# One pool of PSUM banks, matmul waits by pass, a scan tile read in place and a new order: a change to an attention and Mamba-2 kernel

## The chip, the cores and the metric

The kernel runs on one core of one Trainium2 chip. The metric is device time in microseconds (us) for one execution; lower is better. Five engines work side by side, each through its own list of instructions in order: PE (TensorE, matmuls, with its weight loads shown as PEld), DVE (VectorE), ACT (ScalarE), POOL (GpSimd) and SP (SyncE, which here only starts DMAs). They meet through semaphores alone.

## The reference

An image batch of 4 x 128 channels x 32 x 32 goes through two layers. The first is a group norm (8 groups), single-head attention over the 1024 positions with 128 channels, a projection and a residual. The second is a layer norm over channels, a Mamba-2 core, a squeeze-and-excite gate and a residual:

```python
h = _group_norm(x, gn_w, gn_b); q, k, v = split(h @ qkv_w.T + qkv_b)
x = proj(softmax(q k^T / sqrt(128)) v) + x
u = layernorm(x) * norm_g + norm_b;  z, xBC, dt = split(u @ in_w.T)
dt = softplus(dt + dt_bias);  xs, Bm, Cm = split(silu(causal_conv4(xBC) + conv_b))
state = state * exp(dt * A) + (dt * x_t) B_t;   y_t = state C_t      # 1024 steps, 4 heads
y = rmsnorm((y + Dp * xs) * silu(z)) * rms_w;   out = y @ out_w.T
return x + out * sigmoid(se2 @ relu(se1 @ mean(out)))
```

All data is float32.

## The kernel before

**Tiling.** Batches are named a to d. The 1024 positions of a batch are 8 tiles of 128, or two halves of 512. Attention runs over the 8 query tiles: `S` (scores of a tile against one half of the keys, three passes of 512 columns in the faster f32r format, from a high and a low part of each operand: hi x hi, lo x hi, hi x lo), `max` on DVE, `exp` on ACT, `T` (transposes on PE), `pT` (their copy on ACT) and `PV` (on PE). Step numbers run over tile and half: `S5a` is tile 2, half 1 of batch a. `Q` makes the queries of a half, in three passes as well; `q_hi` (ACT) and `q_lo` (DVE) split them into high and low parts.

**Mamba.** The scan over 1024 steps is done in chunks of 128, four in each half. Per half: `UT`, `u` (the normed input, transposed), `InX`, `InBC`, `InZ`, `Dt` (input projections on PE), `conv_*`, `term` and `th_*` (the convolution and silu, on ACT, POOL and DVE), `sp` (nine small DVE steps for softplus), `Cum`, `dec`, `dA`, `DAT` and `l` (the decays), `xdt`, `xend`, `BT`, `G`, `m` (operands and masked scores inside a chunk), `U` (what each chunk adds to the state, PE), `st` (DVE's scan over the four chunks), `stc` (ACT's copy of the scan's result), `Yo` (what earlier chunks give to the output, PE), `Y` (inside the chunk, PE), `yo`, `yo_dx`, `y`, `g` (the sum and the gate), `sq`, `Ss`, `ms`, `y_pow` (the rms norm), `Out`, `o`, `Pl`, `SeA`, `SeB`, `gated`, `fin`, `store`. In batch d the decays come from matmuls (`Dec`, `L`); in a to c they go through DRAM (`wr`, `bc`, `dd` on SP's queue).

**The scan's layout.** `U` writes its bank with a step of four columns, so that the four chunks of one state column lie side by side; `st` scans along them into `scanned[128, 2, 128, 4]`. `stc` (L772) reads that with a step of four elements and writes `stateT[128, 2, 4, 128]`, in which each chunk's state is contiguous. `Yo` (L1333) loads `stateT` as weights, and the second half's `U` (L1317) reads the last chunk of the first half from it, as the moving operand against an identity.

**What sets the order.** One list of step names, `ORDER` (L62 to L138), is written out by hand. Every engine walks the whole list and emits its own steps, so each engine's queue follows that order; the waits of each step are in the code. `name@2` names the PSUM bank that a PE step fills.

**PSUM.** Eight banks: two for `scores` (also the target of `Q`), two `turn` banks for `V` and `T`, one for `attn_out` (`PV`), and three `mamba` banks for all other steps (L175 to L178). `fill` (L378) makes PE wait until the bank's last content was read; it looks this up in two tables, one for each pool.

**Waits of the three passes.** `mm3` (L1159) issues three matmuls in a row. `S` (L1214) and `Q` (L1199) wait for all operands, low parts included, ahead of the first pass.

**Head.** DVE first copies the identity four times (`ident4`), makes `center`, and then the masks that batch d needs (L834 to L842, the last of them behind a wait for all of POOL's constants). Only then do the group norm's statistics of batch a start (`gn_stats`, L883). `gn_dev` is a copy of the group means from PSUM and three small steps (L897 to L900); after `gn_ve` and `gn_pow` comes `gn_aff`, three more (L908 to L910).

## Time and profile before

| what | before |
|---|---|
| three runs | 275.29, 275.69, 276.14 us (median 275.69) |
| the profiled execution's own time | 275.25 us |
| its span, first to last instruction | 273.1 us |
| PE busy | 256.9 us (94%), 1992 matmuls |
| DVE busy | 224.8 us (82%), 517 instructions |
| ACT busy | 208.5 us (76%), 414 instructions |
| POOL busy | 109.0 us (40%), 114 instructions |

PE's busy time is modelled: a matmul's record reaches past the start of the next one, so a PE that is shown busy may still lose some tenths of a microsecond between steps. Where it does, the weight loads (PEld) show an idle time with what ended it. In the profile's rows a line number is a line of the kernel; `L1157` is the helper that issues every matmul, so matmuls are told apart by their tiles (out <- in, moving operand first, weights second). A 32-bit matmul shows as two records, and an f32r matmul as one.

### The profile page before, as it was taken

The numbers are of one execution on the slowest core, as the hardware profiler recorded it, in microseconds if no ns is written. First come the engines' busy times: TensorE is split into PE (matmuls) and PEld (weight loads), VectorE is DVE, ScalarE is ACT, GpSimd is POOL, SyncE is SP. The second block draws the span as 40 slices with busy tenths as digits, with TensorE's granted clock in tenths as the row PEclk, the third lists the DMA queues.
The fourth block names the chain that finished last, engine by engine and source line by source line (L and its number), as shares of the span: only waits on it lengthen the run. The fifth ranks groups of instructions, "written<-read, shape, count | busy, mean of one in ns | idle before, by whom it ended". The sixth has DMA issues, their size and how long they took to land. (4 is left out here: it accounts for less than half of the span.)

```text
span 273.1 us, 6193 instructions
## 1 busy us (share of the span) xinstructions
PE 256.9 (94%) x1992; PEld 224.3 (82%) x1992; DVE 224.8 (82%) x517; ACT 208.5 (76%) x414; POOL 109.0 (40%) x114
## 2 busy tenths in 40 slices
PE   2999999999999999999999998999999999998791
PEld 2889998998888998989989787888889788677680
DVE  5787765754889799889988999999899999599933
ACT  2356579978999887879999875777978888997261
POOL 8030032208053300642387534132463188556162
PEclk9999999999999999999999999999999999999996
DMA  6930000006000600000326000060007201000014
GB/s 175 397 136 4 0 0 4 0 5 186 8 0 6 183 12 2 0 2 0 112 78 206 0 2 1 16 182 2 0 5 189 84 0 42 0 2 1 0 41 155
DMA packets 10987, 15.29 MB, mean 56 GB/s; under 512 B 1515, under 2 KB 5708, under 8 KB 10956
## 3 DMA queue, kind: packets, MB, share of 16 engines
q1 hardware_dynamic: 10412, 14.69, 16.7%
q8 instruction: 17, 0.28, 0.4%
q10 hardware_dynamic: 544, 0.21, 0.3%
q14 instruction: 14, 0.11, 0.2%
HBM read 12.70 MB, written 2.20 MB: 55 GB/s over the span
## 5 line engine op out<-in xcount | busy, mean ns | idle before, releaser
L1157 PEld LDWEIGHTS attn_out<-values,pT 128*128 128x128 f32 x512 | 63.3, 191 | 5.8 <-issue 4.0
L1157 PE MATMUL attn_out<-values,pT 128*128 128x129 f32 x512 | 66.7, 276 | 0.0
L974 DVE TENSOR_REDUCE neg_max<-scores 128x1 f32<-128x1024 f32 x32 | 39.0, 1218 | 16.0 <-PE scores L1157 15.8
L649 ACT ACTIVATE probs<-scores,neg_max 128x512 f32<-128x512 f32 x64 | 41.8, 685 | 13.1 <-DVE neg_max L974 11.1
L655 ACT ACTIVATE pT<-turn 128x512 f32<-128x512 f32 x64 | 37.6, 595 | 10.8 <-PE turn L1230 10.8
L1230 PE MATMUL turn<-ident,probs 128*128 128x128 f32 x256 | 37.1, 273 | 0.0
L575 POOL TENSOR_TENSOR pre<-pre,th 128x512 f32<-128x512 f32 x16 | 21.4, 1336 | 30.0 <-ACT pre L681 18.3
L1230 PEld LDWEIGHTS turn<-ident,probs 128*128 128x128 f32 x256 | 30.2, 142 | 2.9 <-issue 0.7
L1157 PE MATMUL scores<-h_hi,q_hi 128*128 128x512 f32 x64 | 30.4, 474 | 0.0
L1067 DVE TENSOR_TENSOR_SCAN L<-L,ident 128x512 f32<-128x512 f32 x24 | 29.9, 1256 | 0.0
L561 POOL TENSOR_TENSOR ln_rstd<-ln_var,neg_half 128x4 f32<-128x4 f32 x8 | 9.8, 1230 | 47.6 <-DVE ln_var L996 47.5
L1157 PE MATMUL scores<-h_hi,q_lo 128*128 128x512 f32 x64 | 25.3, 395 | 0.0
L1157 PE MATMUL scores<-h_lo,q_hi 128*128 128x512 f32 x64 | 25.1, 392 | 0.0
L1157 PE MATMUL mamba<-u,winC 128*128 128x512 f32 x48 | 24.5, 597 | 0.1
L1081 DVE TENSOR_TENSOR L<-L,mamba 128x512 f32<-128x512 f32 x32 | 21.0, 675 | 0.0
L1013 DVE SCALAR_TENSOR_TENSOR pre<-raw,vec,pre 128x512 f32<-128x512 f32 x21 | 17.8, 849 | 0.1
L582 POOL TENSOR_TENSOR xend<-xdt,to_end 128x512 f32<-128x512 f32 x8 | 8.7, 1089 | 22.0 <-issue 16.5
L588 POOL TENSOR_TENSOR xs<-y,gate 128x512 f32<-128x512 f32 x7 | 10.0, 1423 | 18.4 <-DVE y L1122 18.3
L593 POOL TENSOR_TENSOR y_rstd<-ms,neg_half 128x4 f32<-128x4 f32 x8 | 10.1, 1260 | 15.5 <-DVE ms L1125 15.5
L1157 PEld LDWEIGHTS scores<-h_hi,q_lo 128*128 128x128 f32 x64 | 12.0, 188 | 2.7
L1157 PEld LDWEIGHTS scores<-h_hi,q_hi 128*128 128x128 f32 x64 | 12.1, 189 | 2.6 <-issue 0.9
L776 ACT ACTIVATE stateT<-scanned 128x512 f32<-128x512 f32 x8 | 9.3, 1164 | 5.6 <-DVE scanned L1089 5.6
(219 smaller groups left out, 592.4 us busy)
## 6 DMA issues: line engine op xcount, KB each, us to landing
L<-decay_rows_d SPq DMA_DIRECT2D x24, 256.0 KB, 3.9
res<-in_x_tok SPq DMA_DIRECT2D x4, 512.0 KB, 7.8
out<-res SPq DMA_DIRECT2D x8, 256.0 KB, 2.7
x_all<-in_x SPq DMA_DIRECT2D x3, 512.0 KB, 8.5
decay_in<-decay_rows_d SPq DMA_DIRECT2D x24, 64.0 KB, 3.5
x_all<-in_x SPq DMA_DIRECT2D x2, 256.0 KB, 3.2
winT<-in_in_wT SPq DMA_DIRECT2D x1, 194.0 KB, 7.2
wqkv<-in_qkv_w ACTq DMA_DIRECT2D x1, 192.0 KB, 4.1
```

The lines of the kernel that those rows point to most:

```text
L561: pool.tensor_tensor(ln_rstd[:, four], ln_var[:, four], neg_half[:, four], ALU.pow).then_inc(ln_rstd_ready.sem, 1)
L575: pool.tensor_tensor(pre[:, 1, half_of(n)], pre[:, 1, half_of(n)], term(b, n, j), ALU.add).then_inc(tap["bc"].sem, 1)
L588: pool.tensor_tensor(y2[:, half], y[:, half], gate[:, half], ALU.mult).then_inc(y2_ready.sem, 1)
L593: pool.tensor_tensor(y_rstd[:, four], ms[:, four], neg_half[:, four], ALU.pow).then_inc(y_rstd_ready.sem, 1)
L649: act.activation(probs[:, i % 2, half_of(h)], scores[:, half_of(h)], ACT.Exp, bias=neg_max[:, i:i + 1]).then_inc(exp_done.sem, 1)
L655: act.activation(pT[:, i % 2, QUAD * h:QUAD * (h + 1), :], bank[:, :].rearrange("p (a b) -> p a b", a=QUAD), ACT.Copy).then_inc(pT_ready.s ...
L974: V.tensor_reduce(neg_max[:, n:n + 1], scores[:, :], AX.X, ALU.max, negate=True).then_inc(max_ready.sem, 1)
L1013: V.scalar_tensor_tensor(pre[:, 0, half_of(n)], raw[:, 0, n * HALF + j:(n + 1) * HALF + j], vec[:, CONV_X + j:CONV_X + j + 1], pre[:, 0, h ...
L1067: V.tensor_tensor_scan(chunk, chunk, ident4[:, :, :].rearrange("p a b -> p (a b)"), 0.0, ALU.mult, ALU.add).then_inc(l_ready.sem, 1)
L1081: V.tensor_tensor(M[:, HEADS * n:HEADS * (n + 1), :], L[:, HEADS * n:HEADS * (n + 1), :], bank[:, tile(c)].unsqueeze(1).broadcast_to([P, H ...
L1157: return T.matmul(o, w, v, start=start, stop=stop)
L1230: last = T.transpose(bank[:, tile(c)], probs[:, i % 2, tile(QUAD * h + c)], ident[:, :])
```

## The change

1. **Head.** The masks move out of the head of DVE's list: a new step `masks0` keeps `ident4` and `center`, `masks1` takes the rest and stands behind `q_lo0a`. `gn_dev` reads the group means in PSUM directly, and for batch a fuses two steps; `gn_aff` makes the bias in one step, not two. `kq_ev` moves behind `gn_pow`, `vp_mm` behind the five warm-up matmuls.
2. **Waits by pass.** `mm3` is gone. Each pass of `Q` and `S` has the waits of its own operands: the low part of the keys (`h_lo`) only ahead of the pass that reads it, `q_lo` only ahead of the last.
3. **One pool of banks.** `turn` and `mamba` become five banks for every step, and `Q` fills one of these too, not `scores`. `fill` looks up what read the bank last in one table.
4. **No copies of the states.** `stc` and `stateT` are gone. `Yo` loads its weights from `scanned` with a step of four elements (16 bytes), and the second half's `U` reads its moving operand so; both wait for `st`, and the next batch's `st` waits for `Yo` and `U`.
5. **Order anew.** `ORDER` is rewritten as a whole: the same steps, without `stc` and with `masks`, in another order and with other banks.

On SP's queue the new order puts both halves' `bc` loads ahead of the `dd` loads of batches a and b.

The core of the diff (the order's table shows two lines only):

```diff
@@ ORDER @@
-warm3 gn_stats0 gn_mm10 kq_mm gn_dev0 gn_mm20 kq_ev gn_ve0 vp_mm gn_pow0 gn_aff0 h0a h1a warm5 h_hi0a h_hi1a h_lo0a
+masks0 warm3 gn_stats0 gn_mm10@2 kq_mm@3 gn_dev0 gn_mm20 gn_ve0 gn_pow0 kq_ev gn_aff0 h_hi0a h_hi1a warm5 h0a vp_mm@4
...
-        turn = [ctx.enter_context(nc.psum_tensor(f"turn{k}", [P, HALF], F32)) for k in range(2)]
         attn_out = ctx.enter_context(nc.psum_tensor("attn_out", [P, HALF], F32))
-        mb = [ctx.enter_context(nc.psum_tensor(f"mamba{k}", [P, HALF], F32)) for k in range(3)]
+        pool_banks = [ctx.enter_context(nc.psum_tensor(f"bank{k}", [P, HALF], F32)) for k in range(5)]
...
         def fill(pe, b, kind, n):
-            uses, memory = (TURN_USES, turn) if kind in ("V", "T") else (MAMBA_USES, mb)
+            uses, memory = USES, pool_banks
             bank, before = uses[kind, n, b]
             if before is not None:
...
+                for read, batch, count in released(*before):
+                    wait(pe, read, batch, count)
             return memory[bank], filled[kind].sem
...
-                elif kind == "stc":
-                    wait(act, st_ready, b, n + 1)
-                    wait(act, filled["Yo"], b - 1, n + 1)
-                    wait(act, filled["U"], b - 1, 2)
-                    act.activation(stateT[:, n, :, :], scanned[:, n, :, :].rearrange("s e c -> s c e"), ACT.Copy
-                                   ).then_inc(stc_ready.sem, 1)
...
                 elif kind == "gn_dev":
-                    step_done(V.tensor_copy(gn_mean[:, b0:b1], mb[2][:, b0:b1]))
-                    step_done(V.tensor_tensor(gn_dev[:, b0:b1], gn_mv[:, b0:b1, 0], gn_mean[:, b0:b1], ALU.subtract))
-                    step_done(V.tensor_tensor(gn_dev[:, b0:b1], gn_dev[:, b0:b1], gn_dev[:, b0:b1], ALU.mult))
-                    V.tensor_tensor(gn_dev[:, b0:b1], gn_dev[:, b0:b1], gn_mv[:, b0:b1, 1], ALU.add
-                                    ).then_inc(gn_dev_done.sem, 1)
+                    bank = take(dve, 0, "gn_mm1", n)
+                    step_done(V.tensor_tensor(gn_dev[:, b0:b1], gn_mv[:, b0:b1, 0], bank[:, b0:b1], ALU.subtract))
+                    if n == 0:
+                        V.scalar_tensor_tensor(gn_sq[:, 0:1], gn_dev[:, 0:1], gn_dev[:, 0:1], gn_mv[:, 0:1, 1], ALU.mult, ALU.add
+                                               ).then_inc(gn_dev_done.sem, 1)
...
                 elif kind == "gn_aff":
-                    step_done(V.tensor_tensor(gn_bias[:, b0:b1], gn_mean[:, b0:b1], gn_scale[:, b0:b1], ALU.mult))
-                    V.tensor_scalar(gn_bias[:, b0:b1], gn_bias[:, b0:b1], -1.0, vec[:, GNB:GNB + 1], ALU.mult, ALU.add
-                                    ).then_inc(gn_ready.sem, 1)
+                    for k in range(b0, b1):
+                        last = V.scalar_tensor_tensor(gn_bias[:, k:k + 1], gn_minus_mean[:, k:k + 1], gn_scale[:, k:k + 1],
+                                                      vec[:, GNB:GNB + 1], ALU.mult, ALU.add)
...
                 elif kind == "st":
-                    wait(dve, stc_ready, b - 1, n + 1)
+                    wait(dve, filled["Yo"], b - 1, n + 1)
+                    if n == 0:
+                        wait(dve, filled["U"], b - 1, 2)
...
                 elif kind == "S":
                     i, h = divmod(n, 2)
                     if i == 0:
-                        wait(pe, q_lo_ready, b, h + 1)
+                        wait(pe, q_hi_ready, b, 1)
+                        wait(pe, exp_done, b - 1, 15 + h)
                     else:
                         wait(pe, exp_done, b, n - 1)
+                        wait(pe, q_hi_ready, b, i // QUAD + 1)
+                    wait(pe, h_hi_ready, b, h + 1)
+                    mm(to, q_hi[:, tile(i)], h_hi[:, keys], True, False)
+                    wait_h_lo(pe, b, h + 1)
+                    mm(to, q_hi[:, tile(i)], h_lo[:, keys], False, False)
                     wait(pe, q_lo_ready, b, i // QUAD + 1)
-                    wait_h_lo(pe, b, h + 1)
-                    mm3(scores[:, half_of(h)], q_hi[:, tile(i)], q_lo[:, tile(i)], h_hi[:, half_of(h)],
-                        h_lo[:, half_of(h)]).then_inc(S_filled.sem, 1)
+                    mm(to, q_lo[:, tile(i)], h_hi[:, keys], False, True).then_inc(S_filled.sem, 1)
...
                 elif kind == "U":
                     if n == 1:
-                        wait(pe, stc_ready, b, 1)
+                        wait(pe, st_ready, b, 1)
...
-                        mm(slots[:, 0, :], ident[:, :], stateT[:, 0, QUAD - 1, :])
+                        mm(slots[:, 0, :], ident[:, :], scanned[:, 0, :, QUAD - 1])
...
                 elif kind == "Yo":
-                    wait(pe, stc_ready, b, n + 1)
+                    wait(pe, st_ready, b, n + 1)
                     for c in range(1 - n, QUAD):
-                        last = mm(bank[:, tile(c)], stateT[:, n, c - 1 + n, :], BC[:, tile(QUAD * n + c)])
+                        last = mm(bank[:, tile(c)], scanned[:, n, :, c - 1 + n], BC[:, tile(QUAD * n + c)])
```

The order at three places. The first is the head on DVE, before (`head_mask` and `first` are masks; `gn_*` is the group norm of batch a; `key_query_*` and `col` are `kq_ev`):

```order
L839 TENSOR_TENSOR head_mask<-row_head,row_chunk 128x512
L842 TENSOR_SCALAR first<-ident 128x1
L883 BN_STATS gn_raw<-x_all 128x6 x2
L888 BN_AGGR gn_mv<-gn_raw 128x2
L897 COPY gn_mean<-mamba 128x1
L898 TENSOR_TENSOR gn_dev<-gn_mv,gn_mean 128x1
L899 TENSOR_TENSOR gn_dev<-gn_dev 128x1
L900 TENSOR_TENSOR gn_dev<-gn_dev,gn_mv 128x1
L914 TENSOR_SCALAR key_query_hi<-turn 128x128
L915 SCALAR_TENSOR_TENSOR key_query_lo<-turn,key_query_hi 128x128
L917 TENSOR_SCALAR col<-turn 128x1
L904 TENSOR_SCALAR gn_var<-mamba 128x1
```

and now:

```order
L863 TENSOR_SCALAR center<-ident 128x128
L880 BN_STATS gn_raw<-x_all 128x6 x2
L885 BN_AGGR gn_mv<-gn_raw 128x2
L894 TENSOR_TENSOR gn_dev<-gn_mv,bank 128x1
L896 SCALAR_TENSOR_TENSOR gn_sq<-gn_dev,gn_mv 128x1
L902 TENSOR_TENSOR gn_minus_mean<-gn_dev,gn_mv 128x1
L905 TENSOR_SCALAR gn_var<-bank 128x1
L917 TENSOR_SCALAR key_query_hi<-bank 128x128
L918 SCALAR_TENSOR_TENSOR key_query_lo<-bank,key_query_hi 128x128
L920 TENSOR_SCALAR col<-bank 128x1
L910 TENSOR_SCALAR gn_scale<-gn_rstd,vec 128x1
```

The masks stand ahead of the statistics no more, two small steps are gone ahead of `gn_var`, and `kq_ev` stands behind it.

The second is the same stretch on PE, before (`gn_dev,group_avg` is `gn_mm2`, `wpT` is `vp_mm`, `scores<-ident` are warm-up matmuls, the last three rows are `Q0a`):

```order
L1157 MATMUL mamba<-gn_dev,group_avg 128x1
L1157 MATMUL turn<-wpT,wqkv 128x128
L1157 MATMUL turn<-wpT,vec 128x128
L1157 MATMUL scores<-ident 128x128 x5
L1157 MATMUL scores<-h_hi,key_query_hi 128x512
L1157 MATMUL scores<-h_lo,key_query_hi 128x512
L1157 MATMUL scores<-h_hi,key_query_lo 128x512
```

and now (the last row is `V0a`):

```order
L1163 MATMUL bank<-gn_sq,group_avg 128x1
L1163 MATMUL scores<-ident 128x128 x5
L1163 MATMUL bank<-wpT,wqkv 128x128
L1163 MATMUL bank<-wpT,vec 128x128
L1163 MATMUL bank<-h_hi,key_query_hi 128x512
L1163 MATMUL bank<-h_hi,key_query_lo 128x512
L1163 MATMUL bank<-h_lo,key_query_hi 128x512
L1163 MATMUL bank<-value_proj,h 128x128 x4
```

`vp_mm` stands behind the warm-up matmuls, the pass with the low part of `h` is the last of `Q0a`, and `V0a` stands ahead of `Q1a`.

The third is DVE in batch d behind the last attention step `PV15d`, up to `dt_x1d` (`dtx`), before (`th<-xs,vec,th` is `yo_dx1c`, `y` and `ms` belong to batch c, the rest to d):

```order
L1109 SCALAR_TENSOR_TENSOR th<-xs,vec,th 128x512
L847 CAST dA_rows<-dA 128x32
L849 TENSOR_TENSOR dA_rows<-dA,dA_rows 128x32
L1122 TENSOR_TENSOR y<-mamba,th 128x512
L1125 TENSOR_SCALAR ms<-mamba 128x4
L1051 CAST dA_all<-mamba 128x128
L1052 TENSOR_TENSOR dA_head<-mamba,head_mask 128x512
L1115 SCALAR_TENSOR_TENSOR gate<-gate,zv 128x512
L1000 TENSOR_TENSOR dtx<-mamba,dtb 128x16
L1005 SCALAR_TENSOR_TENSOR dta<-dtx 128x16
```

and now (`L<-L` are `m6c` and `m7c`, `th<-bank,decay_in` is `yo1c`, `x_all` is `gated1b`):

```order
L827 CAST dA_rows<-dA 128x32
L829 TENSOR_TENSOR dA_rows<-dA,dA_rows 128x32
L1085 TENSOR_TENSOR L<-L,bank 128x512 x2
L1055 CAST dA_all<-bank 128x128
L1056 TENSOR_TENSOR dA_head<-bank,head_mask 128x512
L1107 TENSOR_TENSOR th<-bank,decay_in 128x512
L1131 TENSOR_SCALAR ms<-bank 128x4
L1146 SCALAR_TENSOR_TENSOR x_all<-th_att,y 128x512
L1115 SCALAR_TENSOR_TENSOR th<-xs,vec,th 128x512
L1128 TENSOR_TENSOR y<-bank,th 128x512
L1004 TENSOR_TENSOR dtx<-bank,dtb 128x16
```

`m6c`, `m7c`, `yo1c` and `gated1b` stand behind `PV15d` now; `yo1c` was the only one of them behind it before, and `gate0d` moved to behind `dtx`.

## Rows read from the trace of the kernel before

**Rows 1.** Windows, us: busy time (count) of PE, PEld, DVE, ACT, POOL; clock; DMA.

```profile
150.00:226.00 76.00, 74.80 (x617) 65.11 (x616) 73.34 (x158) 60.05 (x121) 32.56 (x28) 1.00 0.15 43
226.00:240.00 14.00, 13.56 (x109) 10.35 (x108) 9.77 (x36) 12.66 (x33) 9.29 (x8) 1.00 0.06 20
240.00:250.00 10.00, 9.19 (x57) 7.48 (x57) 9.88 (x17) 8.91 (x18) 7.24 (x6) 1.00 0.01 2
250.00:262.00 12.00, 9.49 (x122) 7.97 (x122) 11.25 (x19) 4.56 (x9) 2.35 (x3) 1.00 0.00 1
```

**Rows 2.** Longest waits of PE's weight loads, 12 to 226 us: total, times, longest.

```profile
PEld attn_out L1157 <- issue: 4.0, 17, 0.2
PEld mamba L1157 <- issue: 3.5, 15, 0.5
...
PEld mamba L1157 <- ACT stateT L776: 0.9, 1, 0.9
```

**Rows 3.** Timeline of the head: start, us, engine, line, operation [idle before <- releaser].

```profile
4.89 0.15 DVE L842 TENSOR_SCALAR first<-ident 128x1 f32<-128x1 f32 x1 [0.60 <-POOL sp_coef L529]
...
5.08 1.29 DVE L883 BATCH_NORM_STATS2 gn_raw<-x_all 128x6 f32<-128x512 f32 x2
...
7.28 0.16 DVE L897 COPY gn_mean<-mamba 128x1 f32<-128x1 f32 x1 [0.68 <-PE mamba L1157]
...
9.58 2.34 PE L1157 MATMUL scores<-ident 128*128 128x128 f32 x10
...
10.32 1.52 ACT L632 ACTIVATE h_hi<-x_all,gn_bias,gn_scale 128x512 fp32r<-128x512 f32 x2 [5.31 <-DVE gn_bias L910]
...
11.98 0.19 PEld L1157 LDWEIGHTS scores<-h_hi,key_query_hi 128*128 128x128 f32 x1 [0.35 <-DVE h_lo L966]
...
16.26 1.21 DVE L974 TENSOR_REDUCE neg_max<-scores 128x1 f32<-128x1024 f32 x1
```

**Rows 4.** The copied state's tile, `stateT`: duration ns min/median/max, first and last start.

```profile
L1157 PEld LDWEIGHTS mamba<-BC,stateT x56: 186/192/192, 124.2 to 258.3; 128*128 128x128 f32 x56
...
L776 ACT ACTIVATE stateT<-scanned x8: 1121/1161/1203, 122.4 to 256.3; 128x512 f32<-128x512 f32 x8
...
L1157 PE MATMUL mamba<-stateT,ident x8: 275/275/377, 127.2 to 254.1; 128*128 128x128 f32 x8
```

**Rows 5.** Groups by form: busy us, mean ns of one | idle before.

```profile
L1081 DVE TENSOR_TENSOR L<-L,mamba 128x512 f32<-128x512 f32 x32 | 21.0, 675 | 0.0
...
L712 ACT ACTIVATE C<-BC 64x512 f32<-64x512 f32 x8 | 5.0, 629 | 0.2
```

**Rows 6.** Timeline, PE alone: an f32r stream, then loads with one moving column.

```profile
19.59 0.40 PE L1157 MATMUL scores<-h_hi,q_hi 128*128 128x512 f32 x1
...
19.83 0.39 PE L1157 MATMUL scores<-h_lo,q_hi 128*128 128x512 f32 x1
...
264.31 1.93 PEld L1157 LDWEIGHTS mamba<-y_rstd,y 128*128 128x128 f32 x16
```

**Rows 7.** A wait of PE's sequencer by itself, `L1312`: duration ns min/median/max.

```profile
L1312 PEldq EVENT_SEMAPHORE  x8: 51/51/51, 86.2 to 251.1; - x8
```

**Rows 8.** Timeline from the last attention step on, PE and DVE.

```profile
225.75 1.61 PE L1157 MATMUL attn_out<-values,pT 128*128 128x129 f32 x13
...
234.40 0.17 DVE L1000 TENSOR_TENSOR dtx<-mamba,dtb 128x16 f32<-128x16 f32 x1 [1.88 <-PE mamba L1157]
...
234.72 1.10 PE L1157 MATMUL mamba<-u,winC 128*128 128x512 f32 x2
...
236.01 0.18 DVE L855 TENSOR_SCALAR sp_den<-dte 128x16 f32<-128x16 f32 x1 [0.85 <-ACT dte L725]
...
239.56 0.18 DVE L847 CAST dA_rows<-dA 128x32 fp32r<-128x32 f32 x1 [0.57 <-ACT dA L736]
...
257.57 1.16 PE L1157 MATMUL mamba<-BC,stateT 128*128 128x128 f32 x8
...
261.13 0.69 DVE L1131 TENSOR_TENSOR xs<-y,gate 128x512 f32<-128x512 f32 x1
```

313 lines of the change are left out of this document (162 added, 151 removed).

## The prediction

> **What bounds the kernel now.** I read the windows first. From 150 to 226 us, where attention and Mamba steps of three batches run side by side, PE is busy for 74.80 and DVE for 73.34 of 76 us, while ACT (60.05) and POOL (32.56) have room [rows 1]. So PE sets the pace there, with DVE 2 us behind it. Behind 226 us, where the last attention step ends at 225.75 + 1.61 = 227.36 us [rows 8], it is another kernel: DVE is idle for 14 - 9.77 = 4.2 us up to 240 us, and then busy for 21.1 of 22 us up to 262 us [rows 1]. There DVE is the bound, and PE, with 9.49 of 12 us at the end, is not.
>
> Next come PE's own waits, which its modelled busy time hides: weight loads lose 4.0 us in 17 waits ahead of `PV` and 3.5 us in 15 ahead of Mamba steps, each about 0.2 us, and 0.9 us once for the copied state [rows 2]. Last the head: queries start at 11.98 us and the first maximum at 16.26 us [rows 3].
>
> What PE has to do is the same before and after, to the instruction; the change can win only where PE waits, at both ends, and it can lose where a PE instruction gets longer.
>
> **The change, part by part.** I sum against the profiled execution's own 275.25 us, with the 2.15 us around its span left as they are; it lies 0.44 us under the median of the three runs, so I add 0.44 at the end.
>
> *Head.* `first` waits 0.60 us for POOL's last constant and the statistics follow at 5.08 us [rows 3]. Now they can start once the data are there. No row says how early that is, so this is worth 0 to 0.75 us (the wait and the 0.15 us of `first`); I take 0.5. Two of the small steps like `gn_mean` (0.16 us each, 0.2 with the gap, [rows 3]) go ahead of `gn_var`, but PE runs `kq_mm` in that gap anyway, so only 0.1 of the 0.4 us counts; the third, in `gn_aff`, saves 0.2. So `h_hi` starts 0.8 us earlier, at 9.5 instead of 10.32 us. `kq_ev` behind `gn_ve` costs nothing as long as POOL's power (`gn_pow`) takes as long; without that cover it costs its three steps, some 0.6 us. On PE the warm-up (2.34 us, [rows 3]) and `vp_mm` now stand behind `gn_mm2` and ahead of `Q0a`, so its start moves by 0.6 us, not 0.8; `Q0a` no longer waits for `h_lo` (0.35 us, [rows 3]), which is the same time seen from the other side. `masks1` then stands ahead of `max0a` on DVE and takes some of this back, but PE fills that time with `V1a` and `win_mm`, which stood behind it. I take **-0.8 us**, from 0 to -1.2.
>
> *Banks.* With five banks for all, and `Q` out of `scores`, a fill can take a bank that was read long ago. The rows do not say which of the 8.4 us of waits [rows 2] are for a bank and which for data, so this is worth 0 to 8.4 us; a new order makes waits of its own too. Short waits of 0.2 us mean that things come just late, which a freer choice cures often but not always. I take a little over a third, **-3 us**, with the 0.9 us for `stateT` in it.
>
> *No copies.* ACT loses eight copies of 1161 ns [rows 4], 9.3 us; ACT has room, so by itself that is worth nothing but latency, which is counted above. In return 56 weight loads of `Yo` and the 8 matmul records of the second `U` [rows 4] read with a step of 16 bytes. No PE row does this. The nearest by operation are PE's own: an f32r stream takes 19.83 - 19.59 = 0.24 us for 512 columns, 0.47 ns each [rows 6], while one-column matmuls go at the pace of their weight loads, 1.93 / 16 = 0.12 us for 128 columns, 0.94 ns each [rows 6]. If a step of 16 bytes costs two reads for one, there is room for it in a 32-bit load, and the cost is near 0. The nearest by memory is the copy itself: ACT needs 1161 ns for 512 elements with this step and 629 ns for 512 in a row [rows 4, 5], 1.04 ns more for each; 128 of them make 133 ns, and 64 loads 8.5 us. Less than nothing is excluded: a read in steps has no reason to beat one in a row. I take **+0.4 us**, by the PE rows, since the engine is the same, and keep 0 to 8.5.
>
> The Trainium skill (page "SBUF — State Buffer", section "Specifications (TRN2)") speaks against this part: memory lines are 16 bytes, full bandwidth needs at least two hits to a line, and each crossing to a new line pays. ACT's rows agree with it. With PE paying as ACT does, the sum below would be 277.6 us, without a penalty 270.7; that is the first rival.
>
> *Waits by pass.* In batches b to d the pass that reads `h_lo` carries two waits, and one instruction more on PE's sequencer, 51 ns [rows 7]: 48 `S` and 6 `Q`, 2.8 us if none is hidden. The pass before it runs for 0.24 us [rows 6], which covers it unless the sequencer is already late. What it gains is at most 0.35 us at each of four batch starts [rows 3], 1.4 us. I take **+0.3 us**, from -1.4 to +2.8.
>
> *Order.* Behind `PV15d` PE's list now also has `InZ0d` (1.10 us, like the pair in [rows 8]) and `Yo1c` (1.16 us, [rows 8]), while `Cum0d` (four records, 0.5 us at the pace of [rows 6]) stands ahead of it. So the last attention step comes about **1.5 us** earlier, and PE has room for the rest in the 2.5 us that it is idle from 250 to 262 us. DVE there gets `m6c`, `m7c` and `gated1b` more, 2.0 us at 675 ns [rows 5], and loses `gate0d`, which goes behind `dtx`. Their cover is DVE's wait of 1.88 us ahead of `dtx` and the two of 0.85 and 0.57 us behind it [rows 8]; without that cover they cost 2 us at the end, where DVE is the bound. But `Dt1d` stands behind `InX1d` now, so `dtx` is up to 1.1 us later. Filled idle and later start nearly cancel: 0, from -2 to +2. Removing `stc` from the end gives nothing by itself, since DVE is the bound there and `g1d` (261.13 us, [rows 8]) comes when DVE gets to it. On SP the `dd` loads of batches a and b now queue behind both halves' `bc`; `yo` reads them tens of microseconds later, so 0.
>
> Sum: -0.8 - 3 + 0.4 + 0.3 - 1.5 = -4.6. 275.25 - 4.6 + 0.44 = **271.1 us**.
>
> **The rivals.**
>
> *The step of four is paid (slower).* Each of the 64 loads takes 133 ns more. 40 of them lie ahead of `PV15d`, on PE's path: 5.3 us. Of the 24 behind (`Yo1c` 8, `Yo0d` 6, `Yo1d` 8, `U1d` 2) I count half, 1.6 us, as DVE is the bound there. 6.9 instead of 0.4 us: 277.6 us. It decides from about 96 ns for each load on, where 52 loads use up the other parts' 5.0 us. For it speaks ACT's doubled time [rows 4, 5] and that no row shows a 32-bit load of 128 columns go faster than 0.12 us [rows 6], so its spare room is not seen. Against it speaks the f32r stream, twice as fast on the same engine.
>
> *DVE binds instead.* DVE's work is the same but for three small steps, and from 150 to 226 us it has 2.7 us to spare [rows 1]. If it has none at the places where PE now waits less, PE's waits only change their names, and the 3 and the 1.5 us do not come: 275.6 us, no change. Against it: DVE itself waits for PE in places, `dtx` by 1.88 us [rows 8].
>
> *The order does more.* All of the 8.4 us of waits [rows 2] go, not 3: 265.7 us. Against it: that needs every operand on time for each of some 360 PE steps.
>
> *The change doesn't do what it says* is no case here: the order shows the copies gone and the steps moved.
>
> **How the numbers follow.** Forecast 0.52, paid step 0.19, DVE 0.17, more 0.12. A difference under 0.3% (0.8 us) can't be told from no change. Faster: 0.52 and 0.12, and a quarter of the DVE case, 0.68; same: most of the DVE case, 0.11; slower: the paid step and what is left, 0.21. The range goes from 267.0 us, which leaves out most of the third rival, to 277.0 us, which takes in half of the first.
>
> **What would show it.** In the profile after: the first `Q0a` pass at about 11.4 us and the first maximum under 16 us; the `Yo` loads at 192 ns and their matmuls 0.12 us apart (the forecast) or some 0.25 (the first rival); the waits of weight loads between 12 and 226 us down by a third; the last `PV` at about 222 us; from there to the end 45 to 47 us, as before, with DVE over 90% busy in all of its last 30 us. I would be wrong if PE's waits stay at 8 us in all, if `Yo` takes twice its time, or if DVE shows new waits behind `PV15d`.

## The result, and the profile after

| what | before | after |
|---|---|---|
| median (lowest to highest), us | 275.72 (275.29 to 276.14) | 277.71 (277.30 to 278.13) |
| ratio to before, 95% interval | | 1.0072 (1.0051 to 1.0094) |
| span of the profiled execution, us | 273.1 | 275.5 |
| PE busy, us | 256.9 | 261.4 |
| DVE / ACT busy, us | 224.8 / 208.5 | 225.1 / 200.0 |

The change makes the kernel 2.0 us slower. The forecast was 271.1 us, faster; the time lies 0.7 us above the range that was to hold it, and 0.1 us from the first rival's 277.6, which had a chance of 0.19.

PE's busy time is the first sign. It has the same 1992 instructions as before, and is busy for 4.5 us more. So some of its instructions have become longer. The rows of the scan's tile in the changed kernel show which (after the colon: lowest, median and highest duration in ns; then the first and the last start in us):

```profile
L1163 PEld LDWEIGHTS bank<-BC,scanned x56: 307/329/332, 127.2 to 260.5; 128*128 128x128 f32 x56
L1163 PE MATMUL bank<-BC,scanned x56: 270/397/499, 127.6 to 260.6; 128*128 128x128 f32 x56
L1163 PEld LDWEIGHTS bank<-scanned,ident x8: 187/189/208, 122.8 to 256.2; 128*128 128x128 f32 x8
L1163 PE MATMUL bank<-scanned,ident x8: 387/398/407, 123.0 to 256.4; 128*128 128x128 f32 x8
```

[rows 4] had 192 ns for the loads of the copied state and 275 ns for the carry's matmuls. A `Yo` load now takes 329 ns, 137 more, and the matmul behind it follows suit. In the carry the tile is the moving operand: its load (an identity, in a row) is as fast as ever, and the matmul takes 398 ns, 123 more. So both ways of reading pay for the step of four.

The stages of the changed kernel, to be read beside [rows 1] (columns: window; busy us and instruction count of PE, PEld, DVE, ACT and POOL; granted clock; DMA share; GB/s):

```profile
150.00:226.00 76.00, 76.00 (x620) 67.54 (x619) 72.74 (x154) 58.01 (x121) 35.57 (x28) 1.00 0.23 64
226.00:240.00 14.00, 13.62 (x107) 11.09 (x106) 11.69 (x31) 10.90 (x26) 9.96 (x9) 1.00 0.05 20
240.00:250.00 10.00, 9.49 (x62) 7.99 (x60) 8.08 (x23) 9.89 (x23) 5.77 (x5) 1.00 0.01 2
250.00:262.00 12.00, 11.05 (x116) 9.88 (x119) 11.46 (x21) 4.17 (x9) 6.31 (x6) 1.00 0.12 45
```

From 150 to 226 us PE is shown busy without a gap (74.80 before). From 250 to 262 us it is busy for 11.05 us, 1.6 more than before: `Yo0d`, `Yo1d` and the carry lie there.

The last `PV` of the kernel, first before, then after (start, length, engine, line; x16 and x3 are neighbours that the view has joined, two steps in the first two rows). The third row is from a kernel of the experiments, told below:

```profile
225.41 1.95 PE L1157 MATMUL attn_out<-values,pT 128*128 128x129 f32 x16
```
```profile
227.18 2.05 PE L1163 MATMUL attn_out<-values,pT 128*128 128x129 f32 x16 [0.23 <-DVE res L989]
```
```profile
223.16 2.05 PE L1163 MATMUL attn_out<-values,pT 128*128 128x129 f32 x16 [0.23 <-DVE res L989]
```

It ends at 229.23 us, where 222 was forecast and 227.36 stood before. From there to the end it is 46.3 us (45.7 before). So nearly all of the loss has come about by then.

The idle time of PE's weight loads between 12 and 226 us (what waited; for what; us in all, times, longest; "issue" means that the profile names nothing), first the rows of before that [rows 2] did not need, then after:

```profile
PEld turn L1157 <- issue: 1.0, 4, 0.2
PEld scores L1157 <- ACT probs L649: 0.4, 2, 0.2
PEld attn_out L1157 <- DVE res L985: 0.5, 2, 0.3
```
```profile
PEld bank L1163 <- issue: 4.6, 20, 0.2
PEld scores L1163 <- ACT probs L653: 1.6, 5, 0.6
PEld attn_out L1163 <- issue: 1.4, 6, 0.2
PEld bank L1241 <- issue: 1.1, 4, 0.4
PEld attn_out L1163 <- DVE res L989: 0.9, 2, 0.6
```

The waits of `PV` with no named releaser went from 4.0 us in 17 [rows 2] to 1.4 in 6, and the one of 0.9 us for the copied state is gone. Those ahead of steps that fill a bank did not change: 3.5 in 15 [rows 2] and 1.0 in 4 are 4.5 in 19; now it is 4.6 in 20. `S` waits longer for `exp` than before (1.6 against 0.4 us), and `PV` for `res` (0.9 against 0.5).

But most of the short waits with no named releaser are no loss for PE. This is one stretch of the kernel before, on PEld and then on PE (`u,winC` is an input projection of 512 columns, two records):

```profile
150.50 0.42 PEld L1157 LDWEIGHTS mamba<-u,winC 128*128 128x128 f32 x2
151.16 0.19 PEld L1157 LDWEIGHTS attn_out<-values,pT 128*128 128x128 f32 x1 [0.24 <-issue]
151.58 0.53 PEld L1157 LDWEIGHTS attn_out<-values,pT 128*128 128x128 f32 x4 [0.24 <-issue]
```
```profile
150.72 1.02 PE L1157 MATMUL mamba<-u,winC 128*128 128x512 f32 x2
151.58 0.61 PE L1157 MATMUL attn_out<-values,pT 128*128 128x129 f32 x4
```

PE streams the projection from 150.72 to 151.58 us and goes on with `PV` without a gap. The next two loads start 0.43 us apart, as the two records do, and each shows 0.24 us of idle time while PE works; so an idle time of the weight loads alone does not say, as the text ahead of the prediction took it to, that PE loses time. Of the waits with no named releaser, 32 of 49 (7.7 of 11.6 us) before and 31 of 38 (7.6 of 9.2 us) after are such first two loads behind a projection, and PE shows no idle time in any of those before. In [rows 2] they are 14 of the 17 of `PV` and 6 of the 15 of Mamba steps, 4.8 of 7.5 us. Both kernels have the same 48 records of projections; what the new order changed is which step stands behind them, and so whose name the idle time carries.

The head after, on DVE and on PE (beside [rows 3]):

```profile
3.77 0.69 DVE L880 BATCH_NORM_STATS2 gn_raw<-x_all 128x6 f32<-128x512 f32 x1 [0.84 <-DMA x_all<-in_x]
9.40 1.00 DVE L964 TENSOR_SCALAR h<-x_all,gn_scale,gn_bias 128x512 f32<-128x512 f32 x2
15.63 1.23 DVE L978 TENSOR_REDUCE neg_max<-scores 128x1 f32<-128x1024 f32 x1 [0.34 <-PE scores L1163]
```
```profile
10.73 0.77 PE L1163 MATMUL bank<-h_hi,key_query_hi 128*128 128x512 f32 x1
```

The statistics wait for the data alone, `h` (and `h_hi`, at the same time on ACT) starts at 9.40 instead of 10.32 us, `Q0a` at 10.73 instead of 11.98 [rows 3], and the first maximum at 15.63 instead of 16.26. So only half of what `Q0a` gains arrives there: from its first pass to the next step it takes 1.4 us (10.73 to 12.16) where it took 0.8 (11.98 to 12.78), at a granted clock of 1.00 in both traces; why, no run shows. In the kept traces of the seven kernels below that have this head and these waits, the first maximum comes anywhere from 15.07 to 16.03 us.

### The profile page after: what moved, and what is told of

It reads as the page before. It is cut to its first block, busy times and chain, and to the rows that moved or that the text cites. A ratio compares the mean times of both kernels' runs of the same rounds, so it can differ in the third digit from the quotient of the medians.

```text
span 275.5 us, 6187 instructions
## 1 busy us (share of the span) xinstructions
PE 261.4 (95%) x1992; PEld 232.1 (84%) x1992; DVE 225.1 (82%) x516; ACT 200.0 (73%) x406; POOL 112.4 (41%) x114
## 4 chain that ended last, share of the span: by engine, by line
PE 81%; DVE 11%; issue 3%; ACT 2%; POOL 1%; DVEq 0%; ACTq 0%; POOLq 0%
PE bank L1163 34%; PE attn_out L1163 17%; PE scores L1163 17%; PE bank L1241 9%; DVE L L1071 2%; DVE neg_max L978 2%; PE bank L1257 1%; DVE L L1085 1%; PE bank L1309 1%; PE bank L1315 1%; DVE gate L1121 0%; DVE x_all L1146 0%; DVE woutT L936 0%; DVE th L1115 0%; DVE th L1107 0%
## 5 line engine op out<-in xcount | busy, mean ns | idle before, releaser
L659 ACT ACTIVATE pT<-bank 128x512 f32<-128x512 f32 x64 | 37.5, 598 | 19.4 <-PE bank L1241 19.1
L1241 PE MATMUL bank<-ident,probs 128*128 128x128 f32 x256 | 37.4, 273 | 0.2 <-DVE q_lo L974 0.2
L1241 PEld LDWEIGHTS bank<-ident,probs 128*128 128x128 f32 x256 | 30.2, 142 | 2.7 <-issue 1.1
L579 POOL TENSOR_TENSOR pre<-pre,th 128x512 f32<-128x512 f32 x16 | 22.5, 1406 | 24.1 <-ACT pre L685 18.2
L1163 PE MATMUL bank<-u,winC 128*128 128x512 f32 x48 | 24.5, 594 | 0.0
L1085 DVE TENSOR_TENSOR L<-L,bank 128x512 f32<-128x512 f32 x32 | 20.8, 675 | 0.0
L592 POOL TENSOR_TENSOR xs<-y,gate 128x512 f32<-128x512 f32 x7 | 10.7, 1528 | 22.2 <-DVE y L1128 22.2
L559 POOL TENSOR_TENSOR h_lo<-h,h_hi 128x512 fp32r<-128x512 f32 x6 | 7.8, 1313 | 26.1 <-ACT h_hi L636 26.1
L586 POOL TENSOR_TENSOR xend<-xdt,to_end 128x512 f32<-128x512 f32 x8 | 8.7, 1088 | 23.8 <-issue 11.7
L1163 PE MATMUL bank<-BC,scanned 128*128 128x128 f32 x56 | 14.3, 396 | 0.4 <-DVE scanned L1095 0.4
L1163 PEld LDWEIGHTS bank<-BC,scanned 128*128 128x128 f32 x56 | 13.8, 326 | 1.0 <-DVE scanned L1095 0.6
```

What stands on the lines that cost most here:

```text
L579: pool.tensor_tensor(pre[:, 1, half_of(n)], pre[:, 1, half_of(n)], term(b, n, j), ALU.add).then_inc(tap["bc"].sem, 1)
L586: pool.tensor_tensor(xend[:, rows, :], xdt[:, rows, :], to_end[:, rows].unsqueeze(2).broadcast_to([P, R, HEADDIM]), ALU.mult).then_inc(xen ...
L592: pool.tensor_tensor(y2[:, half], y[:, half], gate[:, half], ALU.mult).then_inc(y2_ready.sem, 1)
L659: act.activation(pT[:, i % 2, QUAD * h:QUAD * (h + 1), :], bank[:, :].rearrange("p (a b) -> p a b", a=QUAD), ACT.Copy).then_inc(pT_ready.s ...
L1085: V.tensor_tensor(M[:, HEADS * n:HEADS * (n + 1), :], L[:, HEADS * n:HEADS * (n + 1), :], bank[:, tile(c)].unsqueeze(1).broadcast_to([P, H ...
L1163: return T.matmul(o, w, v, start=start, stop=stop)
```

## The experiments

My theory once the trace was read: the step of four is paid at every read, some 122 ns for each of 56 + 8 records (275 to 397 and 398), 7.8 us of PE's time, and what the rest of the change wins does not make up for it. The main rival: the step's time lies beside DVE's work, and the order or the banks lose the time.

**1. The changed kernel, reading in a row.** `Yo` and the carry read as many elements, 128 that lie side by side:

```diff
-                        last = mm(bank[:, tile(c)], scanned[:, n, :, c - 1 + n], BC[:, tile(QUAD * n + c)])
+                        last = mm(bank[:, tile(c)], scanned[:, n, :, :].rearrange("s e c -> s (e c)")[:, tile(c - 1 + n)],
+                                  BC[:, tile(QUAD * n + c)])
```

> The changed kernel with one difference: Yo and the second U read the first 512 elements of the scan's tile in a row instead of every fourth one (the states are the wrong ones, all else, waits and order too, is the same). Theory: the step of four is what cost the time. In the profile of the changed kernel 56 Yo loads start 0.233 us apart instead of 0.112, and the 8 carry records 0.208 instead of 0.111: 6.8 + 0.8 = 7.5 us of PE's time, of which at least the 40 loads ahead of PV15d and the first carries count in full, the rest half. So 277.7 - 5.5 to 7.5: about 271 us (270.2 to 272.2), loads back at 192 ns. Rival: the step's time lies beside DVE's work, and the new order or its banks lose the time: 276 to 277.7 us although the loads are at 192 ns.

Measured: 272.69 us, ratio to before 0.9896 (0.9861 to 0.9931). The loads are back:

```profile
L1163 PEld LDWEIGHTS bank<-BC,scanned x56: 186/192/192, 127.4 to 256.8; 128*128 128x128 f32 x56
L1163 PE MATMUL bank<-BC,scanned x56: 270/275/377, 127.8 to 256.9; 128*128 128x128 f32 x56
```

So the step cost 277.71 - 272.69 = 5.0 us, give or take one by the two intervals, and without it the change would have been a gain of 2.9 us. The rival falls.

The six runs go from 271.70 to 274.73 us, and the trace is of the slowest. There PE was busy for only 0.91 of 2 us from 222 to 224 us, and then the granted clock fell to 0.50, the lower of its two levels, 1.2 GHz, from 225 to 228 us. The last `PV` took 3.34 us in it:

```profile
224.54 3.34 PE L1163 MATMUL attn_out<-values,pT 128*128 128x129 f32 x16 [0.23 <-DVE res L989]
```

So where the time went is read below from another kernel's trace. The gain is less than the 5.0 us that the prediction's other terms add up to; the later experiments ask where that stayed.

**2. Copies straight behind the scan.** The changed kernel with `stc` back on ACT: behind each `st` of `ORDER` stands its `stc`, and `Yo` and `U` read `stateT`.

```diff
-... st0a raw_x0b ... st1a exp10c ...
+... st0a stc0a raw_x0b ... st1a stc1a exp10c ...
```

> The changed kernel with ACT's copies of the states put back (stc straight behind st on ACT, Yo and U read the copy), all other parts of the change kept. Theory (the step costs, and ACT had room for the copies): about 271 to 272.5 us, since the copies bring back 1.2 us of latency behind each scan, 0.9 us of wait at one place before. Rival (the copies' latency is worth as much as the step): 275 us or more.

Measured: 285.31 us, 1.0368 (1.0331 to 1.0404). Far off both: 12.6 us slower than reading in a row (the trace is of the fastest of its four runs, 283.02 us). ACT goes through its list in order, and `stc` there waits for DVE, which is behind. The first row of that kernel's trace is what `stc` waited for, the others what PE then waited for (12 to 226 us):

```profile
DVE scanned L1096: 11.7, 6
```
```profile
PEld scores L1164 <- ACT probs L650: 4.1, 7, 1.6
PEld bank L1242 <- issue: 4.0, 5, 2.3
```

ACT stood for 11.7 us in six waits, and `exp` and `pT`, which stood behind them, came late: `S` lost 4.1 us waiting for `exp`, where the changed kernel lost 1.6. `T` (L1242) lost 4.0 us in waits with no named releaser, where it had lost 1.1 (L1241 there); it needs `exp` and a bank that `pT` has read. Dropping ACT's copies was not worth nothing, as I had put it; with the order of the change it depends on where they would stand.

**3. The step alone, in the kernel before.** The copies are still made and waited for; only the read changes.

```diff
-                        last = mm(bank[:, tile(c)], stateT[:, n, c - 1 + n, :], BC[:, tile(QUAD * n + c)])
+                        last = mm(bank[:, tile(c)], scanned[:, n, :, c - 1 + n], BC[:, tile(QUAD * n + c)])
```

> The kernel before with one difference: Yo and the second U read the scan's tile with a step of four; the copies are still made and still waited for, so no wait and no place in the order changes. Theory: PE pays 7.5 us more, of which 5 to 7 count: 275.7 + 5 to 7 = 280.7 to 282.7 us. Rival (PE has slack at these places): under 278 us.

Measured: 282.90 us against 275.56, 1.0260 (1.0237 to 1.0283). In the old order the step costs 7.3 us, almost all of its 7.8 us of PE time. The loads show 329 ns there too. So the price does not depend on the order; how much of it is hidden does.

**4. Steps of 1, 2, 3, 4 and 8.** Each step on a line of its own, in the changed kernel:

```diff
+                        T.matmul(bank[:, tile(1)], flat[:, 0:128], BC[:, tile(1)], start=True, stop=True)
+                        T.matmul(bank[:, tile(2)], flat[:, 0:256:2], BC[:, tile(2)], start=True, stop=True)
+                        last = T.matmul(bank[:, tile(3)], flat[:, 0:384:3], BC[:, tile(3)], start=True, stop=True)
...
+                        T.matmul(bank[:, tile(2)], flat[:, 0:1024:8], BC[:, tile(6)], start=True, stop=True)
+                        last = T.matmul(bank[:, tile(3)], flat[:, 512:1024:4], BC[:, tile(7)], start=True, stop=True)
```

> The changed kernel where the reads of the scan's tile use different steps, each on a line of its own (wrong states): Yo's loads with steps of 1, 2, 3 elements in the first half and 1, 2, 8, 4 in the second; the carry's moving operand with steps of 1, 2, 3, 4 in batches a to d. If the price comes from the number of 16-byte lines touched, with two hits to a line being enough: 192 ns at steps 1 and 2, and more at 3, 4 and 8 alike, up to 329. If any step doubles the read: 329 ns at every step but 1. If the price grows with the spread of addresses: 192, about 235, 280, 329 and well over 329 at 8. The moving operand should follow the same pattern.

The loads, with steps of 1 (L1356), 2 (L1357), 3 (L1358), 8 (L1362) and 4 (L1363):

```profile
L1356 PEld LDWEIGHTS bank<-BC,scanned x8: 190/192/192, 127.1 to 251.1; 128*128 128x128 f32 x8
L1357 PEld LDWEIGHTS bank<-BC,scanned x8: 196/197/199, 127.6 to 251.4; 128*128 128x128 f32 x8
L1358 PEld LDWEIGHTS bank<-BC,scanned x8: 252/258/261, 127.9 to 251.6; 128*128 128x128 f32 x8
...
L1362 PEld LDWEIGHTS bank<-BC,scanned x8: 313/324/335, 132.8 to 255.3; 128*128 128x128 f32 x8
...
L1363 PEld LDWEIGHTS bank<-BC,scanned x8: 329/332/333, 133.3 to 255.8; 128*128 128x128 f32 x8
```

At steps of 1, 2, 3, 4 and 8 that is 192, 197, 258, 332 and 324 ns: two is nearly free, three costs half of what four costs, and eight no more than four. This is neither "any step" nor "the spread of addresses". The Trainium skill (page "SBUF — State Buffer", section "Specifications (TRN2)") says that lines are 16 bytes and that full bandwidth needs at least two hits to each; the trace agrees. Read as "an element costs one element time, and a line at least two", 128 elements in steps of 1, 2, 3, 4, 8 touch 32, 64, 96, 128, 128 lines, and take 128, 128, 192, 256, 256 element times. With 192 ns at a step of one and 329 ns at four put in (137 / 128 = 1.07 ns for an element time) that gives 192, 260 and 329 ns at two, three and eight, where 197, 258 and 324 were measured. The moving operand shows the same (steps of 2 and 3 below; 275 in a row and 398 at four are shown above):

```profile
L1340 PE MATMUL bank<-scanned,ident x2: 276/276/277, 170.0 to 170.1; 128*128 128x128 f32 x2
...
L1342 PE MATMUL bank<-scanned,ident x2: 333/338/344, 221.6 to 221.8; 128*128 128x128 f32 x2
```

**5. Copies where ACT is idle.** If the copies of the second experiment hurt only by their place, they can be put elsewhere. In the kernel that reads in a row ACT has idle stretches of one to three microseconds not long behind most scans; each copy of batches a to c goes to one of them or next to it. The first half copies the three chunks that `Yo` needs, the carry and batch d read in steps.

```diff
+                elif kind == "stc":
+                    wait(act, st_ready, b, n + 1)
+                    wait(act, filled["Yo"], b - 1, n + 1)
+                    used = QUAD - 1 + n
+                    act.activation(stateT[:, n, 0:used, :], scanned[:, n, :, 0:used].rearrange("s e c -> s c e"), ACT.Copy
+                                   ).then_inc(stc_ready.sem, 1)
```

> The changed kernel with copies again, but placed by the trace of the kernel that reads in a row: in batches a to c each copy stands where ACT was idle there, some microseconds behind the scan and not straight behind it; the first half copies only the three chunks that Yo reads. The second U reads the scan's tile in steps (2 records a batch), and batch d keeps its reads in steps. Theory (the copies cost 7.6 us in the kernel with copies straight behind the scan because ACT stood waiting for the scan, 11.7 us in 6 waits, and all behind it on ACT with it): 272.7 us of reading in a row, 0.8 to 1.7 for 14 Yo records of batch d, up to 0.8 for the carries: 273.5 us (272.7 to 275). Rival (the copies themselves are in ACT's way, 6 of about 1.1 us, or the latency of 1.2 us is): over 277 us.

Measured: 273.86 us, 0.9920 (0.9894 to 0.9946). It leaves nothing out and beats both kernels: 1.9 us under the 275.79 us of before in these runs, 3.9 under the changed one. The copies take as long as ever, but the wait for the scan is gone from their rows (what the copies waited for, below the row):

```profile
L777 ACT ACTIVATE stateT<-scanned x6: 918/1031/1131, 118.1 to 227.2; 128x384 f32<-128x384 f32 x3, 128x512 f32<-128x512 f32 x3
its engine sat idle before it (us, times) until:
  issue: 0.5, 2
```

**6. One pool in the old order.** The changed code under the list of before, copies at their old places, masks at the head; each fill gets the bank of the five that was read longest ago in the list.

```diff
-stats0c term2b max5c stc0a PV4c Yo0a@1 Cum0b@2 pT5c gate0a exp10c PV5c sp11b pT6c T7c@0 T8c@1 cd0b sp12b
+stats0c term2b max5c stc0a PV4c Yo0a@0 Cum0b@1 pT5c gate0a exp10c PV5c sp11b pT6c T7c@2 T8c@3 cd0b sp12b
```

> The code of the changed kernel (one pool, waits by pass, the shorter steps of the head) under the order of before, masks at the head, copies at their old places; the banks are given by rule, each fill the one of five that was read longest ago in the list. So no new order and no step. Prediction's terms: banks -2.1 without the 0.9 for the copied state, waits +0.3, small head steps -0.3: about 273.5 us (271.5 to 274.5). Rival (in the old order the waits are for data, not for banks): 275.6 us, no change.

Measured: 277.13 us, 1.0049 (1.0032 to 1.0066): no gain, but 1.3 us lost. The waits (12 to 226 us):

```profile
PEld bank L1164 <- issue: 5.3, 17, 1.3
PEld attn_out L1164 <- issue: 3.3, 14, 0.2
PEld bank L1316 <- issue: 1.4, 1, 1.4
```

With five banks free to all, `PV` still waits 3.3 us in 14 (4.0 in 17 before), and steps that fill a bank wait no less than before. Most of the short waits are the loads behind a projection, told above, which no choice of banks can cure. The two long ones, 1.4 and 1.3 us, are new, and PE's own rows name what ended them:

```profile
91.86 0.52 PE L1316 MATMUL bank<-ident,BC 128*128 128x128 f32 x3 [0.96 <-DVE q_lo L977]
172.72 0.46 PE L1164 MATMUL bank<-BC,stateT 128*128 128x128 f32 x2 [0.92 <-ACT pT L656]
```

In this kernel's list `BT1a` fills the bank that `Q0c` filled last, and `q_lo0c` on DVE still had to read it; `Yo0b` fills the bank of `T1d`, which `pT1d` on ACT had to read. Neither step needs these results for anything else. So, read from the list and these rows, the rule that gave out the banks made two waits for banks, and together they are more than the 1.3 us lost.

**7. Waits ahead of the first pass again.** Experiment 1, with all waits of `S` and `Q` ahead of their first pass (the diff shows `S`):

```diff
                     wait(pe, h_hi_ready, b, h + 1)
+                    wait_h_lo(pe, b, h + 1)
+                    wait(pe, q_lo_ready, b, i // QUAD + 1)
                     mm(to, q_hi[:, tile(i)], h_hi[:, keys], True, False)
-                    wait_h_lo(pe, b, h + 1)
                     mm(to, q_hi[:, tile(i)], h_lo[:, keys], False, False)
-                    wait(pe, q_lo_ready, b, i // QUAD + 1)
```

> The kernel of the first experiment (the changed one that reads in a row, wrong states) with the waits of S and Q put back ahead of the first pass. Prediction's term for waits by pass is +0.3 us from -1.4 to +2.8, so against 272.7 us: 272.4 (269.9 to 274.1). Rival: the new order counts on them, so that passes start before h_lo and q_lo are there and undoing costs more than 1.4 us: over 274.1 us.

Measured: 273.31 us, 0.9907 (0.9886 to 0.9929). Undoing them costs 0.6 us, give or take about one by the two intervals. So waits by pass can't be told from no change here; a cost of 0.3 us is not excluded.

**8. The step in batch d alone.** Batches a to c read in a row (as in experiment 1, not each chunk's own state), d in steps.

```diff
-                        last = mm(bank[:, tile(c)], scanned[:, n, :, c - 1 + n], BC[:, tile(QUAD * n + c)])
+                        last = mm(bank[:, tile(c)], scanned[:, n, :, :].rearrange("s e c -> s (e c)")[:, tile(c - 1 + n)]
+                                  if by_dma(b) else scanned[:, n, :, c - 1 + n], BC[:, tile(QUAD * n + c)])
```

> The changed kernel where only batch d reads the scan's tile in steps; a to c read in a row (wrong states). 14 Yo records at 121 ns and 2 of the carry at 97 ns more: 1.9 us of PE behind the last attention step. The prediction counted such reads by half, as DVE is the bound there: 272.7 + 0.9 = 273.6 us. If DVE hides them all: 272.7. If they lie on the path in full: 274.6. The reads of a to c then carry the rest of the 5.0 us that the step cost in all.

Measured: 273.74 us, 0.9947 (0.9924 to 0.9970), 1.05 us above reading in a row. That is half of the 1.95 us of batch d's 16 records (122 ns each), as the prediction had counted, but with the scatter of both kernels (272.98 to 275.45 us here) it may be none or all. The traces part the price better; their granted clock is 1.00 up to 262 us. Up to the last `PV` this kernel reads in a row, and that ends at 223.16 + 2.05 = 225.21 us (third row of the `PV` rows above), 4.0 us before the changed kernel's 229.23; 0.25 of this was there at the first maximum (15.38 against 15.63 us). From the last `PV` to the end it is 45.6 us, 46.3 in the changed kernel, where `Yo1c` is read in steps too, and 44.9 and 44.7 in experiments 7 and 10, where all is read in a row. So about 3.8 us of the price lie ahead of the last `PV`, some 0.7 are `Yo1c`'s and some 0.8 batch d's; together they are 5.3, near the 5.0 us of experiment 1.

**9. The old order with two pools.** Experiment 6 with the pools and bank numbers of before, `Q` in `scores` again.

```diff
-                    bank, done = fill(pe, b, "Q", n)
+                    wait(pe, exp_done, b - 1, 15 + n)
+                    bank, done = scores[:, half], filled["Q"].sem
```

> The kernel of the sixth experiment with the two pools and the bank numbers of before, and Q in scores again; waits by pass and the shorter head steps stay (the first S of each half still waits for q_lo, which reads that bank). If the one pool, with banks chosen by rule, is what cost 1.3 us in the old order: 275.0 to 275.8 us. If the waits by pass or the edited head cost it: 276.5 to 277.5 us, as in the sixth experiment.

Measured: 275.55 us, 0.9997 (0.9978 to 1.0015). Against before, waits by pass and the shorter small steps of the head (masks still at the front) change nothing that can be measured. Against experiment 6, one pool with banks given by this rule costs 1.6 us. The two waits for banks shown there, 2.7 us, are not in this kernel's trace, whose longest wait of that kind is 0.5 us.

**10. The head of before.** Experiment 1 with DVE's masks at the front and the longer chain of small steps. I put the wait for all of POOL's constants ahead of all the masks, not only ahead of the last of them, so this head is later than that of before (statistics at 6.35 us, not 5.08).

```diff
                 elif kind == "masks":
-                    dve.wait_ge(consts_done.sem, 1)
+                    dve.wait_ge(consts_done.sem, 9 + TERMS)
```

> The kernel of the first experiment (reads in a row, wrong states) with the head of before: the masks at the front of DVE's list behind all of POOL's constants, gn_mean copied, gn_dev and gn_aff in single steps, kq_ev ahead of gn_ve, vp_mm ahead of gn_pow. The prediction gave the head 0.8 us (0 to 1.2): 272.7 + 0.8 = 273.5 us (272.7 to 273.9), with the first maximum about 0.7 us later. Rival (the time won in the head is lost again later, since PE's later waits take it up): 272.7 us although the first maximum comes later.

Measured: 275.15 us, 0.9989 (0.9963 to 1.0016), 2.5 us above experiment 1.

```profile
6.35 1.29 DVE L876 BATCH_NORM_STATS2 gn_raw<-x_all 128x6 f32<-128x512 f32 x2
11.61 1.00 DVE L955 TENSOR_SCALAR h<-x_all,gn_scale,gn_bias 128x512 f32<-128x512 f32 x2
```

`h` starts 2.2 us later (11.61 against 9.41 in experiment 1), the first maximum 1.2 us (17.22 against 16.03) and the end 2.5 us, give or take one. So time lost in the head is not won back later, and the rival falls. It is no exact undoing of the change's head, and how much of that head's 0.9 us reaches the end is not shown: at the first maximum it is 0.63 us in the changed kernel, and 0.2 to 1.2 in the other kernels' traces.

**11. The first half of batch d copied too.** Experiment 5, with `stc0d`, `U1d` ahead of `Yo0d`, and `yo0d` behind the second scan.

```diff
-... G1d@2 Yo0d@0 xend1d bt1d gated1c m4d fin0c U1d@4 yo0d yo_dx0d st1d Y0d@0 ...
+... G1d@2 xend1d bt1d stc0d gated1c m4d fin0c U1d@4 Yo0d@0 st1d yo0d yo_dx0d Y0d@0 ...
```

> The kernel of the fifth experiment (copies where ACT is idle) with the first half of batch d copied too, its U1 ahead of Yo0, and yo0 behind the second scan on DVE; only Yo1d still reads in steps. In the kernel that reads in a row ACT is idle for 5.7 us behind the first scan of d, so the copy costs nothing there, 6 Yo records save 0.7 us, and U1d comes 0.7 us earlier. If that lies on the path: 273.9 - 0.4 to 1.0, about 273.2 us. Rival (yo0d behind the scan makes Y0d and all behind it later, or DVE hides it): 273.9 us or up to 275.

Measured: 273.93 us, 0.9927 (0.9907 to 0.9947), the same as experiment 5. The rows of the scan's tile, first in experiment 5, then in 11 (the last number of a row's times is the last start):

```profile
L1166 PEld LDWEIGHTS bank<-BC,scanned x14: 309/330/332, 251.0 to 256.8; 128*128 128x128 f32 x14
L1098 DVE TENSOR_TENSOR_SCAN scanned<-chunk_decay,bank x8: 1199/1208/1214, 114.7 to 253.9; 128x512 f32<-128x512 f32 x8
```
```profile
L1098 DVE TENSOR_TENSOR_SCAN scanned<-chunk_decay,bank x8: 1201/1208/1221, 115.2 to 252.6; 128x512 f32<-128x512 f32 x8
L1166 PEld LDWEIGHTS bank<-BC,scanned x8: 309/329/332, 255.5 to 257.1; 128*128 128x128 f32 x8
```

The second scan starts at 252.6 instead of 253.9 us, yet the last load of `Yo1d`, which reads it, comes at 257.1 instead of 256.8. In PE's list `Y0d` stands between, in the bank that `yo0d` reads, and I had moved `yo0d` behind the scan: the time won by the scan is taken by that wait. (That is read from the code; no run parts the two.)

**12. Less work for DVE.** Experiment 1, with half of the masked scores `m` left out in batches b and c.

```diff
-                    V.tensor_tensor(M[:, HEADS * n:HEADS * (n + 1), :], L[:, HEADS * n:HEADS * (n + 1), :],
-                                    bank[:, tile(c)].unsqueeze(1).broadcast_to([P, HEADS, P]), ALU.mult
+                    heads = HEADS // 2 if b in (1, 2) else HEADS
+                    V.tensor_tensor(M[:, HEADS * n:HEADS * n + heads, :], L[:, HEADS * n:HEADS * n + heads, :],
+                                    bank[:, tile(c)].unsqueeze(1).broadcast_to([P, heads, P]), ALU.mult
```

> The kernel of the first experiment (reads in a row, wrong states) with half of DVE's masked scores left out in batches b and c: 16 instructions of 675 ns become half as long, some 5.4 us less on DVE in the stretch where attention and Mamba steps run side by side; PE's work is unchanged. If PE alone sets the pace there, as the prediction's forecast has it: 272.7 us (272.0 to 273.4). If DVE binds at many places, as its second rival has it, and this is where the expected gain of banks and order stayed: 271 us or less, up to 5.4 us off.

Measured: 271.70 us, 0.9856 (0.9820 to 0.9892): 1.0 us less than experiment 1, between the two theories; its interval overlaps that of experiment 1. The steps did not become half as long:

```profile
L1086 DVE TENSOR_TENSOR L<-L,bank 128x512 f32<-128x512 f32 x16 | 10.3, 675 | 0.0
L1086 DVE TENSOR_TENSOR L<-L,bank 128x256 f32<-128x256 f32 x16 | 6.3, 408 | 0.0
```

16 steps at 408 instead of 675 ns are 4.3 us less on DVE, not 5.4. The waits with no named releaser ahead of bank fills are 5.6 us in 22 with the lighter DVE, as in experiment 1, so this work of DVE does not make them. That DVE sets the pace in places is possible, but 1.0 us within this scatter does not show it.

## Why the prediction was wrong, point by point

| term | forecast, us | what the runs showed |
|---|---|---|
| step of four | +0.4 (0 to +8.5) | +5.0 in the new order (1), +7.3 in the old (3) |
| banks | -3 (0 to -8.4) | no gain seen: 4.8 of the 7.5 us priced are loads behind a projection; +1.6 in the old order (6, 9) |
| order, and tail | -1.5, 0 | -1.3 from the first maximum to the last `PV` (8 against before); tail 45.7 before, 44.7 to 44.9 in a row (7, 10) |
| waits by pass | +0.3 (-1.4 to +2.8) | -0.6, within the scatter (7) |
| head | -0.8 (0 to -1.2) | `h_hi` 0.92 us earlier, first maximum 0.63; not won back later (10) |
| all but the step | -5.0 | -2.9 (1) |

**The step that failed** is the choice between the two bounds for the step of four. The bounds held: the price is 5.0 us of the 8.5, and a load takes 137 ns more, where ACT's rows gave 133. I chose the lower one "by the PE rows, since the engine is the same": an f32r stream reads a column in half the time of a 32-bit load, so I took the load to have time to spare for a second read. It has, but that is not enough. A step of two touches twice the lines of a read in a row and takes 197 ns; a step of four touches four times as many and takes 332 (experiment 4). The rival's own argument, that no row shows a 32-bit load go faster, and ACT's rows were the right guide. ACT and PE pay nearly the same for an element (1.04 and 1.07 ns); whether the memory that they share or a port of each engine sets this price, no run shows. Of the miss of 6.6 us this step is 4.6.

**How it was counted** held. The rival put 40 loads on the path and half of 24 behind it. By the traces of experiment 8 about 3.8 us lie ahead of the last `PV` (5.3 foreseen) and some 1.5 us behind it (1.6 foreseen). That the total then met 277.6 almost exactly is partly luck: the step cost less than its 6.9 us, and the rest won less than its 5.0.

**Banks** were the second miss, 2.1 us together with the other terms. The prediction read [rows 2]'s idle times as PE's own waits, put them down to banks or data without a row that said which, and took a third of them. 4.8 of the 7.5 us with no named releaser are the first two loads behind a projection, while PE streams; no bank could win them. With five banks for all they are as many and as long as before, in the old order (experiment 6) and in the new. `PV`'s part of them fell with the new order since other steps stand behind the projections now, and that by itself wins nothing. Where a bank did make PE wait, in experiment 6, it was one that the new pool shared out badly. The gain of 2.9 us fits the other terms: in the trace of experiment 8 the first maximum is 0.9 us earlier than before, and the last `PV` a further 1.3 us, near the 1.5 that the prediction gave to steps moved behind it. No run parts order, banks and the copies' latency in this 1.3.

**ACT's copies** were costed as worth nothing but latency. Experiment 5, with six of them back and 1.9 us gained on before, is in line with that. But experiment 2 shows what I had not asked: in a list that was written without them, the same copies cost 12.6 us against reading in a row when they stand where ACT must wait for DVE.

**What was to show it.** First `Q0a` pass at 10.73, earlier than the 11.4 foreseen; first maximum at 15.63 (under 16): right. `Yo` loads at 329 ns: the first rival. Waits down by a third: wrong, all rows of that view (0.2 us and more) add up to 15.3 us before and 13.0 after, 15% less, and half of it and more lay under PE's streaming. Last `PV` at about 222: wrong, 229.2, and 225.2 without the step ahead of it. 45 to 47 us from there: right. DVE over 90% busy in all of the last 30 us: wrong, it has 8.08 of 10 us from 240 to 250. New waits of DVE behind `PV15d` were a sign of being wrong: there `yo` waits 0.8 us for PE, and `pooled` 1.4 us longer, while waits of 0.8, 0.6 and 0.4 us of before are gone.
